# Three instead of four experts on all tokens in the head, one instead of two at the end, sixty instead of fifty-eight sparse, and ScalarE dividing the probabilities of six attention steps

## The reference

```python
def L3_xattn(q, kv, seg_id, ...):              # b = 4, lq = 256, H = 16 heads of 128
    scores = (q_nope @ k_nope + q_rope @ k_rope) * scale
    good = (k_ids <= qs) & (k_ids >= qs - LOOKBACK)
    attn = softmax(where(good, scores, NEG))
    return (attn @ v).reshape(b, lq, H * HD) @ W_o

def L3_ffn(hidden_states, gate_w, gate_proj_w, up_proj_w, down_proj_w):   # E = 64, K = 8, I = 96
    router_logits = x @ gate_w
    routing_weights, selected = top_k(router_logits, K)
    routing_weights = softmax(routing_weights)
    # for each token its 8 experts: down(silu(gate(x)) * up(x)), weighted and summed
    out = sum(out_of_expert * routing_weights)
```

## Time and profile before

| | |
|---|---|
| median of 3 runs | 686.11 us (685.12 to 688.25) |
| the profiled execution's own time | 685.7 us |
| its span in the trace | 683.0 us |
| PE busy | 609.0 us, 89% of the span |
| VectorE busy | 523.7 us, 77% |
| ScalarE busy | 428.1 us, 63% |
| GpSimd busy | 363.0 us, 53% |
| mean granted TensorE clock | 0.977 |
| the chain that ended last | PE 59%, DVE 19%, POOL 8%, ACT 7%, issue 6% |

### The profile page before, as it was taken

How to read it: one execution, slowest core, us unless ns; L and a number is a source line. 1 busy time by engine, 2 the same in 40 slices (tenths; PEclk the granted TensorE clock), 3 DMA queues, 4 the chain that set the end, 5 groups by cost and what they waited for, 6 DMA issues and landing times.

```text
span 683.0 us, 14285 instructions
## 1 busy us (share of the span) xinstructions
PE 609.0 (89%) x4996; PEld 508.8 (74%) x5000; DVE 523.7 (77%) x1534; ACT 428.1 (63%) x1150; POOL 363.0 (53%) x524
## 2 busy tenths in 40 slices
PE   3998979898899879989999999897799989988877
PEld 3977867776589834668888878675599888888764
DVE  6494489989856788687778988778778878878466
ACT  3635578949745368767776666452358878868430
POOL 6615848964600225435543888677405665666620
PEclk9999999999999999999999999999799999999998
DMA  8999023200010050039300112534448878876384
GB/s 318 334 300 300 27 58 106 82 2 1 4 47 1 0 231 1 2 95 368 114 2 10 66 67 83 183 135 154 159 146 280 261 263 292 282 251 216 133 344 168
DMA packets 47701, 100.50 MB, mean 147 GB/s; under 512 B 7390, under 2 KB 27951, under 8 KB 46246
## 3 DMA queue, kind: packets, MB, share of 16 engines
q1 hardware_dynamic: 40374, 82.33, 36.0%
q0 software_dynamic: 7248, 17.18, 6.8%
HBM read 60.04 MB, written 43.12 MB: 151 GB/s over the span
## 4 chain that ended last, share of the span: by engine, by line
PE 59%; DVE 19%; POOL 8%; ACT 7%; issue 6%; another core or an unknown queue 0%; DMA 0%; DVEq 0%; ACTq 0%; POOLq 0%
PE bank L349 13%; PE bank L351 12%; PE bank L350 11%; PE bank L2650 4%; PE bank L3707 3%; PE bank L2668 3%; PE bank L2658 2%; POOL hl L1238 2%; DVE st L382 2%; DVE HN L402 2%; DVE pt L1451 1%; DVE nm L1459 1%; PE bank L3790 1%; PE bank L1574 1%; POOL raw L1329 1%
## 5 line engine op out<-in xcount | busy, mean ns | idle before, releaser
L3946 POOL DMA_INDIRECT rows_out<-ye,di x87 | 91.4, 1051 | 65.0 <-issue 19.3
L3357 POOL DMA_INDIRECT slots_in<-row,si x64 | 65.6, 1026 | 25.1 <-issue 17.2
L349 PE MATMUL bank<-x7h,w7h 128*96 128x192 f32 x232 | 63.0, 272 | 10.5 <-DVE h L3885 5.7
L2839 POOL TENSOR_SCALAR p6n<-p6n,ri6n 128x128 f32<-128x128 f32 x120 | 46.1, 401 | 46.2 <-DVE ri6n L2785 45.8
L349 PE MATMUL bank<-w7h,h7h 96*128 96x256 f32 x164 | 49.7, 303 | 14.8 <-DVE X L3496 9.4
L351 PE MATMUL bank<-x7h,w7l 128*96 128x192 f32 x232 | 59.1, 255 | 0.3 <-issue 0.2
L350 PE MATMUL bank<-x7l,w7h 128*96 128x192 f32 x232 | 59.0, 254 | 0.0
L2715 ACT ACTIVATE p6n<-sc6n,mn6n 128x128 f32<-128x128 f32 x128 | 50.4, 397 | 10.8 <-DVE mn6n L2762 10.4
L396 POOL TENSOR_TENSOR rs<-ve,neghalf 128x2 f32<-128x2 f32 x32 | 23.1, 721 | 59.4 <-DVE ve L390 59.1
L3180 DVE TENSOR_TENSOR w7l<-w7f,w7h 128x640 fp32r<-128x640 f32 x60 | 49.5, 826 | 4.2 <-issue 2.3
L349 PEld LDWEIGHTS bank<-x7h,w7h 128*96 128x96 f32 x232 | 38.0, 164 | 13.9 <-DVE w7l L3180 8.9
(11 more groups left out here) (483 smaller groups left out, 2247.0 us busy)
## 6 DMA issues: line engine op xcount, KB each, us to landing
w7f<-in_w SPq DMA_DIRECT2D x64, 320.0 KB
xe<-slots_in SPq DMA_DIRECT2D x29, 432.0 KB
slots_in<-zt SPq DMA_DIRECT2D x7, 1728.0 KB, 17.9
rows_out<-zt SPq DMA_DIRECT2D x8, 1024.0 KB, 11.1
rw<-rows_out SPq DMA_DIRECT2D x3, 2048.0 KB
w0raw<-in_w SPq DMA_DIRECT2D x3, 768.0 KB
wo<-in_w_o SPq DMA_DIRECT2D x1, 2048.0 KB
raw<-in_w SPq DMA_DIRECT2D x2, 704.0 KB
```

The costliest lines, as they stand in the source:

```text
L349: T.matmul(out, lh, rh, start=first, stop=False, **kw)
L2839: a = G.tensor_scalar(p, p, m.ri6n[q % 5][:, i:i + 1], 1.0, ALU.mult, ALU.mult)
L3357: G.indirect_dma_start(out=m.buf_in, out_offset=bass.IndirectOffsetOnAxis(ap=m.si7[:, t, j:j + 1], axis=0), in_=m.row7[:, t, :], in_offset ...
L3946: G.indirect_dma_start(out=m.buf_out, out_offset=bass.IndirectOffsetOnAxis(ap=m.di7[:, q:q + 1], axis=0), in_=m.ye7[q % NY][:], in_offset= ...
```

## The change

`FIRST, LAST = 3, 63`: experts 0 to 2 run dense in the head (six passes), 3 to 62 sparse (sixty, thirty pairs), and 63 dense at the end (two passes). One slot of memory for small weights goes (`w7h3`), two buffers of `rw7` move up by 5120 bytes, the zero fill's last block grows from four to eight experts' rows (432 to 864 KB), and the tail's passes and sums are put in an order for two passes. In the attention, steps q = 18, 20, ... 28 (`by_scalar`) are divided by ScalarE with a scale by pointer, at k = 2q + 6 behind the exponentials of that k, instead of by GpSimd at k = 2q + 5; `normalized(k)` picks the semaphore that PE waits for. One split of expert weights fewer stands in the attention, at k = 24 and 25. The diff (the same edit of the splits in the fallback attention, which doesn't run, is left out):

```diff
@@ -25,7 +25,7 @@
 FAR = -float(2.0 ** 100)
 E7 = 64
 CAP = 192
-FIRST, LAST = 4, 62
+FIRST, LAST = 3, 63
 LOWS = 5
 ROW = 288
 S8, W8, BASE = D, D + 8, D + 16
@@ -280,10 +280,6 @@
     m.ng7, m.sm7, m.r7 = [a(n, [P, NT]) for n in ("ng7", "sm7", "r7")]
     m.top7, m.fit7 = a("top7", [1, 1]), a("fit7", [1, 1], I32)
     assert a.at <= rest
-    a = Room(nc, sixth)
-    m.w7h.append(a("w7h3", [P, 640], F32R))
-    both(m.w7f, m.w7l, a, 3)
-    assert a.at <= seventh
     a = Room(nc, top)
     m.ex7, m.mr7 = a("ex7", [P, 4, 64]), a("mr7", [P, 4, 64])
     m.eq7 = [a(f"eq7{i}", [P, 8, E7]) for i in range(2)]
@@ -304,9 +300,9 @@
     m.pick7 = [a(f"pick7{i}", [P, 2, 6, 8]) for i in range(2)]
     m.di7 = a("di7", [P, 3 * (LAST - FIRST) // 2], U32)
     assert a.at <= top + 5120
-    a = Room(nc, rest)
+    a = Room(nc, rest + 5120)
     m.rw7 = [a(f"rw7{i}", [P, NT, 2, D]) for i in range(2)]
-    assert a.at <= rest + 7 * 5120
+    assert a.at <= rest + 8 * 5120
     a = Room(nc, rest + NW * 5120 + 12 * 2048)
     m.rw7.append(Room(nc, a.at + NX * 3 * ROW * 4)("rw72", [P, NT, 2, D]))
     m.rw7.append(a("rw73", [P, NT, 2, D]))
@@ -2594,6 +2590,8 @@
     sc, mn, ri, tr, pt, pn = [sig(n, c) for n, c in (
         ("scores", 32), ("masked", 64), ("recip", 32), ("probs_T", 32), ("probs_T_sbuf", 32), ("probs_p", OWN))]
     ex, pnv = sig("exps", 64), sig("places", 32 - OWN)
+    by_scalar = tuple(range(18, OWN, 2))
+    pna = sig("probs_scalar", len(by_scalar))
     pv, oh, ol, y = [sig(n, 32) for n in ("heads", "heads_hi", "heads_lo", "heads_out")]
     m.heads_read = ol.at(32)
     m.queries_done, m.y_done = qlat.at(32), y.at(32)
@@ -2650,8 +2648,14 @@
                     i = T.matmul(B[2 + s][:, c], m.Q6[k % 2][r, j, c], K[r, w], start=(j == 0), stop=(j == 1))
         i.then_inc(sc.sem, 1)
 
+    def normalized(k):
+        if k >= OWN:
+            return pnv.at(k + 1 - OWN)
+        done = sum(q <= k for q in by_scalar)
+        return pna.at(done) if k in by_scalar else pn.at(k + 1 - done)
+
     def tensor_turn(k):
-        T.wait_ge(*(pn.at(k + 1) if k < OWN else pnv.at(k + 1 - OWN)))
+        T.wait_ge(*normalized(k))
         if k >= 1:
             T.wait_ge(*pt.at(k))
         for i in range(4):
@@ -2732,6 +2736,13 @@
                 A.copy(m.op6h[q % 2][:], B[6][:, 0:256]).then_inc(oh.sem, 1)
             if 3 <= k < 64:
                 scalar_exp((k - 3) // 2, (k - 3) % 2)
+            if k % 2 == 0 and (k - 6) // 2 in by_scalar:
+                q = (k - 6) // 2
+                A.wait_ge(*ri.at(q + 1))
+                for i in range(4):
+                    a = A.activation(m.p6n[q % 5][:, i, :], m.p6n[q % 5][:, i, :], ACT.Copy,
+                                     scale=m.ri6n[q % 5][:, i:i + 1])
+                a.then_inc(pna.sem, 1)
             if k >= 26:
                 g, ago = routing(k)
                 if ago == 6:
@@ -2740,7 +2751,7 @@
                     r.scalar_exps(g)
                 if ago == 11:
                     r.scalar_high(g)
-            if k in (12, 16, 20, 24):
+            if k in (12, 16, 20):
                 w7.scalar_high(k // 4 - 3)
 
     def vector_query(q):
@@ -2831,14 +2842,14 @@
     def gpsimd():
         r.gpsimd_small()
         for k in range(74):
-            if 5 <= k < 5 + 2 * OWN and k % 2:
+            if 5 <= k < 5 + 2 * OWN and k % 2 and (k - 5) // 2 not in by_scalar:
                 q = (k - 5) // 2
                 G.wait_ge(*ri.at(q + 1))
                 for i in range(4):
                     p = m.p6n[q % 5][:, i, :]
                     a = G.tensor_scalar(p, p, m.ri6n[q % 5][:, i:i + 1], 1.0, ALU.mult, ALU.mult)
                 a.then_inc(pn.sem, 1)
-            if k in (13, 17, 21, 25):
+            if k in (13, 17, 21):
                 w7.gpsimd_low(k // 4 - 3)
             if k == 24:
                 r.gpsimd_places()
@@ -3768,10 +3779,7 @@
                 if k == ns + 9:
                     T.wait_ge(*hid.at(ns))
                 dense_up(i, (half,))
-        dense_up(2)
-        dense_down(0)
-        dense_up(3)
-        for q in (1, 2, 3):
+        for q in range(nl):
             dense_down(q)
         for n in (3, 2, 1):
             tensor_sum(n)
@@ -3916,8 +3924,9 @@
             if k >= 1:
                 q = k - 1
                 dense.vector_add(q, LAST + q // 2, q % 2, ns + 2 * q, x, lambda t: 4 * (q - 2) + t % 4 + 1 if q >= 2 else 0)
-            if k >= 2:
-                vector_sum(nl + 1 - k)
+            if k:
+                vector_sum(4 - k)
+        vector_sum(1)
         V.wait_ge(*red.at(5))
         V.wait_ge(*dense_done(7))
         V.tensor_tensor(m.X[:, by_vector, :], m.X[:, by_vector, :], m.rw7[3][:, by_vector, 0, :],
@@ -4033,7 +4042,7 @@
 
     loads = FIRST + NW
     for s in range(8):
-        value[f"load{s}"] -= 16 * ((E7 - loads) // 8)
+        value[f"load{s}"] -= 16 * len([e for e in range(loads, E7) if e % 8 == s])
     value["w7_hi"] -= E7 - FIRST - 8
     value["w7_lo_v"] -= E7 - FIRST - LOWS
     return value
```

## The result

The change makes the kernel slower: 699.0 us (695.3 to 700.0, four runs) against 686.5 (685.1 to 688.3), ratio 1.0166 with a 95% interval of 1.0132 to 1.0200. The forecast was 683.2, the range 678.5 to 687.5.

A forecast was written before the change was run, and what follows sets the result against it. PE work was taken as the price nearly everywhere, with transfers also holding the head's and tail's seams. Terms 0 (attention) - 3.6 (head) + 5.0 (sparse) - 3.9 (tail) = -2.5 from 685.7 gave 683.2 us, range 678.5 to 687.5.

The forecast's parts named there:

- The attention, 0: Attention's later part: moving four multiplications in six steps from GpSimd to ScalarE changes nothing; near bound +0.5 us.
- The slower rival: Attention: ScalarE's four added operations become the bound, each of six steps pays 1.2 us, +7.2, total 690.4; chance 0.10.
- my bounds of 1.2 and 1.6: Attention: ScalarE's four added operations cost between 1.2 and 1.6 us a step.
- The argument of free time: Attention: ScalarE's waits for PE leave 1.16 us free a step, and the following step pays back the 0 to 0.4 overrun.
- The head, -3.6: Head: two of eight dense passes go, but the scatter chain sets the seam; -3.6 us, bounds -5.6 to -1.1.
- the 1.0: Head: the last scatter's 1.95 us wait for PE shrinks with fewer passes ahead, taken as -1.0 us.
- The `HTl` wait, nothing: Head: pass 3's wait for VectorE's `HTl` replaces an earlier PE wait; 0 to +2.5, covered by 3.6 us of slack.
- The sparse stage, +5.0: Sparse stage: two more sparse experts at 2.49 us each, +5.0 us; 4.5 below, 5.2 above.
- the half clock that I had put into the head at +1.0: Start of the sparse stage: PE's idling lowers its granted clock to 0.50 for 5 us, +1.0 (0 to +2.5).
- The tail, -3.9: Tail: two of four dense passes go, the last sum then waits for the rows; -3.9 us, bounds -6.1 to -3.0.
- The program's start, 0: Start: the zero fill of `slots_in` grows by 432 KB, hidden because nobody waits for the loads behind; otherwise +1.3 us.
- two of three cases of mine: Cases: forecast 683.2 (0.55); more at both seams 677.6 (0.20); both seams capped at half clock 686.8 (0.15); ScalarE-bound 690.4 (0.10).

The follow-up runs named there:

- first pair of traces: Profiled executions of the changed kernel and the kernel before, from the first timing: 699.0 us against 686.5, ratio 1.0166.
- third call: Long chip, against the kernel before (682.9 us): division alone 1.0195; new expert numbers, GpSimd dividing 1.0007; ScalarE dividing, GpSimd four spare multiplications 1.0014; nobody dividing 694.3 us.
- second call: Long chip: the change once more against the kernel before (684.9 us), 1.0108; and the kernel before once more for its trace, one run, 680.0 us.

## Why the prediction was wrong

**The attention, 0: the step that failed.** "GpSimd's 1.6 us a step go from an engine that stood 46.2 us ... no gain" costed the removal by GpSimd's own time. It never asked what stands behind the multiplications in its queue: scatters, which then close up. On the long chips that is 12.4 us in the first pair of traces, 2.1 for each of the six steps, and 13.3 by the times of the division alone. The trace of before doesn't price a row of five: in its attention one stands only behind the last multiplications. But it had the sign, in the three copies of `Q` that came 1.1 to 1.5 us after PE behind rows of three.

**The slower rival** had the sign and the place, at 690.4, but not the cause. ScalarE's four divisions took 1.27 us, between my bounds of 1.2 and 1.6, and where nobody is held up behind GpSimd's row they cost nothing: 1.0014 on a long chip, 0.9997 on a short one. The argument of free time held: from 374 to 440 us ScalarE's waits for PE ahead of `Q` and `op6h` are 12.1 us with GpSimd dividing and 8.0 with ScalarE dividing and GpSimd busy (both of the third call).

The Trainium skill (ScalarE: Activation LUTs, What ACT_TABLE_LOAD costs) agrees with the 1.27 better than my estimate from it, 1.17, which took the overlap of 93 ns off all four operations. The last has none behind it: three of 293 and one of 386 ns are 1.26 us, an estimate from the same page.

**The head, -3.6.** -3.7 in the first pair of traces, by the mechanism named: the first load of `xe` is issued behind the last scatter, and PE waits 5.2 us for it. The timelines of SyncE and PE in the changed kernel:

```profile
503.23 12.53 SPq L3676 DMA_DIRECT2D xe<-slots_in  x7
...
506.56 1.54 PE L3718 MATMUL bank<-ident,xe 128*128 128x128 f32 x6 [5.23 <-DMA xe<-slots_in]
```

It lands in 3.3 us, as taken from the store. But the last scatter still waited for PE (1.79 us at 500.72), so nothing of the 1.0 came. The agreement belongs to this pair of traces. In the second call's, on another long chip, the head is 44.5 us against 46.7, and the kernel before began its first transposes 3.9 us after it issued the load. With 3.3 for the load its slack was 0.6 us and not 3.6. On a short chip the first transposes are at 488.6 with the new experts and at 488.3 with the old, where the load was issued at 484.7: PE and the scatters' chain ended there within 0.3 us, and the two passes are worth nothing.

**The `HTl` wait, nothing.** It is there with 5.1 us, and is covered, as said, by the slack that the scatters leave PE.

**The sparse stage, +5.0.** +6.1, and +5.8 on a short chip (120.7 against 114.9). Two things make it. The tenth to the sixtieth experts' transposes are 123.57 us apart, 2.47 each, against 119.32 from the tenth to the fifty-eighth before: +4.25 for the two more. The first nine take 13.66 instead of 11.69 us, +2.0, at the half clock that I had put into the head at +1.0. On the short chips the same stretch is 13.4 us without and 11.7 with the spare matmuls. Window of the changed kernel, to be held against the earlier trace rows:

```profile
506.00:511.00 5.00, 4.44 (x23) 4.44 (x24) 1.11 (x2) 0.96 (x2) 0.00 (x0) 0.54 0.96 340
```

PE had waited 5.2 us before. By the Trainium skill (TensorE: Matmul & The Clock Gate, Part 1, The HAM clock gate) the halved clock is the default state, which activity lifts; the 0.54 behind that wait agrees with it.

**The tail, -3.9.** Only -2.0. The mechanism held: PE waits for `rw` three times, and last for the piece that ends it all. Timeline of SyncE, PE and ScalarE, changed kernel, against the earlier trace rows:

```profile
677.30 0.32 SPq L3702 DMA_DIRECT2D rw<-rows_out  x1
...
688.19 1.13 PE L3798 MATMUL bank<-rw,ident 128*128 128x512 f32 x2 [1.21 <-DMA rw<-rows_out]
...
691.08 0.37 ACT L3848 COPY X<-bank 128x256 f32<-128x256 f32 x1 [21.91 <-PE bank L3799]
```

The missing part is the last load's way and what follows it. The load is issued 33.3 us behind the last transposes, 32.8 before. PE's last sum begins 10.9 us behind it (688.19 - 677.30), where I had taken 8.5 to 9 from issue to landing. The copy begins 2.9 later, near the 2.6 taken at full clock, but 4.7 ahead of the end (695.8 - 691.08) instead of 3.8: the last store of `out` is issued at 691.96, 3.8 ahead of it, and was issued at 680.09 before, 2.9 ahead. On a short chip the tail gains nothing: 49.9 us against 49.2.

**The program's start, 0.** No run here takes the larger zero fill out by itself. The first copy of `Q` is at 295.9 after and 296.7 before, so nothing is lost inside the span up to there; whether the 1.2 us outside the span belong to it is open.

**The sum without the attention** was -2.5. The run that shows it is the new numbers of experts with GpSimd dividing: 1.0007 on a long chip, +0.5 us, and 1.0103 on a short one, +7 us. On the long chips the terms that were mis-sized are the tail (1.9 us), the sparse stage (1.1) and what lies outside the span (1.2, put at nothing). On the short one the old numbers of experts leave PE busy all through the sparse stage, and two more sparse experts and the half clock ahead of them are paid in full (+5.8), while head (-0.3 from `rs` to the first transposes) and tail (+0.7) hang on transfers. Window of the run with the division alone on the short chip, against 108.44 of 119.40:

```profile
500.00:603.00 103.00, 103.00 (x1012) 103.00 (x1011) 95.77 (x255) 98.70 (x264) 71.26 (x69) 1.00 0.92 307
```

The chance of 0.09 for slower was too small in any case: two of three cases of mine took their gain from slack of a few us at seams whose other side was a chain of transfers.

## What to carry to other kernels

Work taken from an engine that isn't the bound still changes when everything behind it in its queue is issued. If that is a train of indirect DMAs, look at how they lie against the other engines' signals before costing the removal at nothing. Where a stage's start is set by two chains within a few us of each other, a gain from shortening one of them is worth the gap between them, and that gap differs from chip to chip (3.6 and 0.6 us on two long ones, 0.3 or less on a short one).

## What the runs showed of the hardware

- The same program takes 656 us on two chips and 683 to 687 on the others, at a granted clock that hardly differs (0.984 and 0.977). The first 296 us are alike (first copies of `Q` at 295.0 and 296.7); the difference lies where GpSimd issues indirect DMAs, most of it in the sparse stage, 114.9 against 131.3 us (the short chip's figures are from the run with the division alone, 0.9997 of before). That the scatters are its cause isn't shown; each chip was seen in one or two calls.
- On the long chips, a row of five indirect DMAs of about 1.26 us each goes with copies on ScalarE that begin 1.8 to 2.6 us after the PE work they wait for, near the row's end, and a row of three with 1.1 to 1.5 us. Four multiplications (1.42 us) in the row remove the loss (1.0014), one (0.4 us) about half of it (1.0093), a bare wait nothing (1.0174).
